# An attention layer over a graph: first layers of the radial network on quarters of TensorE, the odd aggregation in another bank

## The chip, the cores and the metric

The kernel runs on one core of a Trainium2 chip, in one launch. The metric is device time in microseconds (us), the median of repeated runs. A core has TensorE (PE, matrix products into PSUM banks), VectorE (DVE), ScalarE (ACT), GpSimd (POOL), SyncE (SP), and 16 DMA engines. Each engine takes its instructions in order; engines wait for one another through semaphores.

## The reference

400,000 edges, sorted by target node, join 12,500 nodes of 128 channels. For each edge a message is made, weighed by a softmax over the edges of its target, and summed there:

```
h = max(layernorm(x), 0)
msg_src = h @ w_src + b_src;  msg_dst = h @ w_dst
message = msg_src[src] + msg_dst[dst]
rad     = silu(silu(attr @ w1 + b1) @ w2 + b2) @ w3 + b3        # 32 -> 64 -> 64 -> 128
message = message * edge_weight * rad
message = message @ w_sep + b_sep                               # 8 heads, 16 for alpha, 16 for value
score   = sum(smooth_leaky_relu(alpha) * alpha_dot)             # per head
att     = segment_softmax(score, dst)
out     = x + segment_sum(value * att, dst) @ w_proj + b_proj
```

All of it is in float32.

## The kernel before

A first part (to about 235 us) makes the node tables `msg_src` and `msg_dst` and tables of indices and masks. A last part (from about 4935 us) divides the sums and projects them. Between them is the edge loop, which is the case here.

The loop goes over tiles of 512 edges: 832 tiles, one a step, written out in full (`stream`). Steps are grouped by 16 (`G`), and a group has one softmax. Two steps, an even and an odd one, make a pair `k`; the radial network is computed once a pair, for 1,024 edges. Each engine has its own function `step(g, j)` for step `j` of group `g`, and what stands there in order is the order on the engine. There is no scheduler. `there(t)` says whether tile `t` exists; `later(g, j, d)` is `d` steps on. The weighed sum of a tile comes 30 steps (`LAG`) after its message, when the softmax of its group is known. The names of the work:

- GpSimd: four gathers a step (L1057), each 128 rows of `msg_src` into `gath`, by indirect DMA. `gath` has four buffers, so the gathers of step t wait for the transposes of step t - 4 (`s_xT`).
- TensorE, in each step: transposes of `gath` into `xT_ps` (L1347) on top of the product that placed the target rows there the step before (`dst_part`, L1293); `aggregate` of tile t - 30 (L1304); every fourth step `scores` (L1314, four products side by side, 32 columns of the array each); the alpha half of the message, `a_ps` (L1366); its value half, `v_ps` (L1374); `dst_part` for the next step. Of the radial network, `z1` (L1270) is the first layer: one of its two products each step, behind the transposes. `z2` (L1276), the second layer, stands at the end of the even step, and `radial` (L1282), the third, in the odd step behind `a_ps`, as two products on upper and lower half of the array's rows.
- The weights `w1` and `w2` are laid out as blocks on a diagonal of 64x64 blocks with zeros elsewhere, so a full 128x128 product serves two sets of edges and half of the array multiplies by zero.
- ScalarE: `first` and `second` are the silu behind layers one and two, `measure` and `prepare_hotT` make the selection matrix for `dst_part`, `copy_values` empties `v_ps`, and `sil` (L1243) is the silu on `a_ps`.
- VectorE: `msgT` (L1176) multiplies the message by `rads`; `scale_rad` (L1122) makes `rads` from the third layer; `mark` (L1132, `hot`) makes the selection matrix for the aggregation, in even steps; `weigh` (L1145, `wval`) makes weight times value, twice in odd steps; `accumulate` (L1164, L1167, `run`) adds the aggregation into the running sums; `sil` (L1197); and the pieces of the softmax (`soft`), in even steps.

PSUM: `z_ps` has two banks, the first for layer one and the second for layer two. `rad_ps` has two banks for the third layer; `aggregate` writes the first 272 columns of the first of them in even steps and of the second in odd ones, and so `radial` has to wait until VectorE has taken the odd tile's sums (`s_run`).

## Time and profile before

| what | us |
|---|---|
| median of 3 runs (lowest, highest) | 5045.86 (5043.74, 5046.71) |
| the profiled execution | 5048.61 |
| its span, first to last instruction | 5046.1 |
| TensorE busy | 4810.6 (95%) |
| VectorE busy | 3892.4 (77%) |
| GpSimd busy | 3696.0 (73%) |
| ScalarE busy | 2640.2 (52%) |
| edge loop, first to last gather | 235.1 to 4822.9 |

Busy is the time in which an instruction of the engine ran. For TensorE, products are pipelined and the ends are modelled; the distance from one start to the next says more than the duration. For GpSimd, "issue" stands for idle time in which it waited for nothing that the profile shows. An engine that is idle, and is not the one that all wait for, costs nothing.

### The profile page before, as it was taken

What the parts mean: (1) busy time and instruction counts of PE and PEld (TensorE: products, weight loads), DVE (VectorE), ACT (ScalarE), POOL (GpSimd) and SP (SyncE); (2) the same over time, 40 slices, a digit from 0 to 9 for tenths busy, and PEclk for the clock granted to TensorE, in tenths of its full rate; (3) what the DMA queues carried; (4) which work ended last, traced back from release to release, by engine and by line L of the source; (5) the groups of instructions that cost most, each with busy time, mean ns of one, the idle gap of its engine ahead of it and who ended that gap; (6) DMA issues with size and microseconds to landing.
All of it is one profiled execution on the core that took longest, in us unless ns stands there. A gap on an engine that the chain in (4) does not pass through costs nothing. (4 is left out here: it accounts for less than half of the span.)

```text
span 5046.1 us, 92924 instructions
## 1 busy us (share of the span) xinstructions
PE 4810.6 (95%) x28995; PEld 3437.8 (68%) x28995; DVE 3892.4 (77%) x6981; ACT 2640.2 (52%) x3992; POOL 3696.0 (73%) x3491
## 2 busy tenths in 40 slices
PE   3599999999999999999999999999999999999975
PEld 2456777777777777777777777777777777777764
DVE  6547877878777787877877787787777778777777
ACT  2455555555555555555555555555555555555521
POOL 2377777777777777777777777777777777777716
PEclk9799999999999999999999999999999999999975
DMA  6666766666666666667666676766666666666635
GB/s 188 191 200 199 211 208 208 208 208 208 201 212 210 208 205 210 205 203 214 208 208 204 208 209 202 213 207 210 206 206 209 203 213 206 209 207 206 210 79 159
DMA packets 889683, 1019.25 MB, mean 202 GB/s; under 512 B 161781, under 2 KB 778009, under 8 KB 888864
## 3 DMA queue, kind: packets, MB, share of 16 engines
q1 hardware_dynamic: 758843, 774.32, 47.5%
q0 software_dynamic: 108784, 223.44, 18.1%
q10 hardware_dynamic: 21556, 15.50, 1.2%
q8 instruction: 233, 3.82, 0.3%
q14 instruction: 267, 2.18, 0.1%
HBM read 863.59 MB, written 152.34 MB: 201 GB/s over the span
## 5 line engine op out<-in xcount | busy, mean ns | idle before, releaser
L1057 POOL DMA_INDIRECT gath<-msg_src,idx x3328 | 3553.2, 1068 | 1064.6 <-issue 964.9
L1243 ACT ACTIVATE sil<-a_ps,ba 128x512 f32<-128x512 f32 x832 | 572.0, 688 | 1671.0 <-PE a_ps L1366 1670.2
L1374 PEld LDWEIGHTS v_ps<-wv,msgT 128*128 128x128 f32 x6656 | 835.4, 191 | 526.3 <-issue 526.3
L1304 PEld LDWEIGHTS rad_ps<-wval,hot 128*128 128x128 f32 x6656 | 905.3, 193 | 74.0 <-DVE wval L1145 30.5
L1304 PE MATMUL rad_ps<-wval,hot 128*128 128x136 f32 x6656 | 923.0, 282 | 27.8 <-DVE wval L1145 26.5
L1176 DVE TENSOR_TENSOR msgT<-xT_ps,rads 128x512 f32<-128x512 f32 x832 | 575.2, 691 | 455.9 <-PE xT_ps L1347 410.5
L1374 PE MATMUL v_ps<-wv,msgT 128*128 128x128 f32 x6656 | 924.1, 282 | 0.0
L1366 PE MATMUL a_ps<-msgT,wa 128*128 128x512 f32 x1664 | 878.9, 610 | 9.1 <-DVE msgT L1176 9.1
L1122 DVE SCALAR_TENSOR_TENSOR rads<-rad_ps,b,rows_bc 128x1024 f32<-128x1024 f32 x416 | 534.1, 1284 | 294.8 <-PE rad_ps L1282 294.8
L1293 PE MATMUL xT_ps<-hotT,win 128*128 128x256 f32 x3328 | 731.3, 342 | 0.0
L1197 DVE SCALAR_TENSOR_TENSOR sil<-a_ps,sil 128x512 f32<-128x512 f32 x832 | 568.8, 684 | 208.0 <-ACT sil L1243 207.8
L1228 ACT ACTIVATE vals<-v_ps 128x512 f32<-128x512 f32 x832 | 493.8, 594 | 339.9 <-PE v_ps L1374 321.3
L1293 PEld LDWEIGHTS xT_ps<-hotT,win 128*128 128x128 f32 x3328 | 481.1, 190 | 199.9 <-issue 199.9
L1145 DVE TENSOR_TENSOR wval<-vals,wT 128x544 f32<-128x544 f32 x832 | 596.5, 717 | 0.4 <-ACT wT L1240 0.4
L1270 PE MATMUL z_ps<-attr,w 128*128 128x256 f32 x1664 | 499.0, 382 | 29.8 <-DMA attr<-in_edge_attr_t 29.8
L1132 DVE TENSOR_TENSOR hot<-iota_row,rel_tab 128x1024 f32<-128x1024 f32 x416 | 505.7, 1216 | 0.0
L1347 PE MATMUL xT_ps<-ident,gath 128*128 128x128 f32 x3328 | 499.2, 272 | 0.0
L1219 ACT ACTIVATE apart<-rows_bc,row_below 128x1024 f32<-128x1024 bf16 x416 | 473.5, 1138 | 12.7 <-DMA win<-msg_dst 12.7
L1282 PE MATMUL rad_ps<-h,w 64*128 64x512 f32 x1664 | 470.6, 642 | 0.2 <-DVE run L1167 0.2
L1223 ACT ACTIVATE hotT<-apart 128x1024 fp32r<-128x1024 f32 x416 | 441.8, 1062 | 0.0
L1276 PE MATMUL z_ps<-h,w 128*128 128x512 f32 x832 | 426.8, 595 | 0.0
L1347 PEld LDWEIGHTS xT_ps<-ident,gath 128*128 128x128 f32 x3328 | 383.7, 140 | 0.0
(235 smaller groups left out, 4059.2 us busy)
## 6 DMA issues: line engine op xcount, KB each, us to landing
rows_bc<-edge_rows SPq DMA_DIRECT2D x416, 768.0 KB
win<-msg_dst SPq DMA_DIRECT2D x1664, 128.0 KB
sums<-run SPq DMA_DIRECT2D x416, 272.0 KB
attr<-in_edge_attr_t SPq DMA_DIRECT2D x1664, 32.0 KB
gath<-msg_src,idx POOLq DMA_INDIRECT x3328
msg_dst<-dst_parts SPq DMA_DIRECT2D x98, 128.0 KB, 2.1
pen_g<-pen_rows SPq DMA_DIRECT2D x208, 32.1 KB
mask_g<-mask_rows SPq DMA_DIRECT2D x208, 32.0 KB
```

Of the source, the lines that this page charges most:

```text
L1057: pool.indirect_dma_start(gath[:, u, s], None, msg_src, bass.IndirectOffsetOnAxis(ap=idx[:, j // 8, at:at + 1], axis=0)).then_inc(s_gath[u ...
L1122: dve.scalar_tensor_tensor(rads[:, j % 4:j % 4 + 2].rearrange("p n (i e) -> p (n i) e", i=2), rad_ps[:, :, :].rearrange("p n (i e) -> p (n ...
L1132: dve.tensor_tensor(hot[:, u:u + 2].rearrange("p n s q -> p (n s) q"), iota_row[:, :].unsqueeze(1).broadcast_to((P, 2 * SUB, P)), rel_tab[ ...
L1145: product = dve.tensor_tensor(wval[:, u], vals[:, slot], wT[:, :, at:at + H].unsqueeze(3).broadcast_to((P, SUB, H, HV)), ALU.mult)
L1176: dve.tensor_tensor(msgT[:, j % 2], xT_ps[:, :], rads[:, j % 4], ALU.mult).then_inc(s_msg, 1)
L1197: dve.scalar_tensor_tensor(sil[:, j % 8], a_ps[:, :], 0.25, sil[:, j % 8], ALU.mult, ALU.add).then_inc(s_al, 1)
L1243: act.activation(sil[:, j % 8], a_ps[:, :], ACT.Silu, bias=ba[:, :]).then_inc(s_sil, 1)
L1293: last = pe.matmul(xT_ps[:, cols], lhsT=win[:, j % U, i, n], rhs=hotT[:, j % 4, cols], start=(i == 0 and n == 0), stop=False, skip_group_c ...
L1304: last = pe.matmul(rad_ps[:, j % 2, AW * i:AW * (i + 1)], lhsT=hot[:, j % 4, s], rhs=wval[:, j % 4, s].rearrange("p h k -> p (h k)"), star ...
L1347: last = pe.matmul(xT_ps[:, s * P:(s + 1) * P], lhsT=gath[:, j % U, s], rhs=ident[:, :], is_transpose=True, start=False, stop=True, skip_g ...
L1366: pe.matmul(a_ps[:, :], lhsT=wa[:, :], rhs=msgT[:, q], start=True, stop=True).then_inc(s_a, 1)
L1374: last = pe.matmul(v_ps[:, s * P:(s + 1) * P], lhsT=msgT[:, q, s * P:(s + 1) * P], rhs=wv[:, :], start=True, stop=True)
```

## The change

- `z1` computes the whole first layer of a pair in one go, in the even step: four products on quarters of the array (64 rows by 64 columns), 256 columns of edges each, without the zero blocks. `z2` does the same for the second layer. Both stand behind the even step's aggregation, `z2` first.
- The outputs are laid out anew: each bank of `z_ps` holds layer one in columns 0 to 255 and layer two in columns 256 to 511. `h1` and `h2` swap their shapes, and the two silu of ScalarE read both banks.
- `radial` moves in the odd step from behind `a_ps` to behind the aggregation.
- The odd aggregation writes the second bank of `z_ps` instead of the second of `rad_ps` (`partial`). TensorE waits ahead of the aggregation for the running sums of the tile before, and in the odd step also for `first` of the next pair (`layers_read`), which has read that bank.
- ScalarE does `second` and then `first` in the even step, ahead of `sil`; both were in the odd one, on either side of it.
- VectorE does `scale_rad` ahead of the second `weigh` instead of behind it, and waits there for `rows_bc` too.

On TensorE, in the loop's middle. Before, from an even step's scores to the next odd step's `v_ps` (`rad_ps<-h,w` is the third layer, `rad_ps<-wval,hot` the aggregation, `z_ps<-attr,w` the first layer, `z_ps<-h,w` the second):

```order
L1314 MATMUL sc_ps<-sil,adot 32x512 x4
L1366 MATMUL a_ps<-msgT,wa 128x512
L1374 MATMUL v_ps<-wv,msgT 128x128 x4
L1276 MATMUL z_ps<-h,w 128x512
L1293 MATMUL xT_ps<-hotT,win 128x256 x4
L1347 MATMUL xT_ps<-ident,gath 128x128 x4
L1270 MATMUL z_ps<-attr,w 128x256
L1304 MATMUL rad_ps<-wval,hot 128x136 x4
L1366 MATMUL a_ps<-msgT,wa 128x512
L1282 MATMUL rad_ps<-h,w 128x512 x2
L1374 MATMUL v_ps<-wv,msgT 128x128 x4
```

and now, from an odd step's transposes to the next even step's `a_ps` (`z_ps<-wval,hot` is the odd aggregation):

```order
L1364 MATMUL xT_ps<-ident,gath 128x128 x4
L1321 MATMUL z_ps<-wval,hot 128x136 x4
L1299 MATMUL rad_ps<-h,w 128x512 x2
L1390 MATMUL a_ps<-msgT,wa 128x512
L1395 MATMUL v_ps<-wv,msgT 128x128 x4
L1310 MATMUL xT_ps<-hotT,win 128x256 x4
L1364 MATMUL xT_ps<-ident,gath 128x128 x4
L1321 MATMUL rad_ps<-wval,hot 128x136 x4
L1286 MATMUL z_ps<-h,w 64x256 x4
L1277 MATMUL z_ps<-attr,w 64x256 x4
L1331 MATMUL sc_ps<-sil,adot 32x512 x4
L1390 MATMUL a_ps<-msgT,wa 128x512
```

The two halves of the first layer and the second layer leave their places, and stand as two sets of four behind the aggregation of the even step; the third layer stands ahead of `a_ps`; the odd aggregation goes to `z_ps`.

On VectorE, the odd step, from one `msgT` to the next. Before:

```order
L1176 TENSOR_TENSOR msgT<-xT_ps,rads 128x512
L1145 TENSOR_TENSOR wval<-vals,wT 128x544
L1164 SCALAR_TENSOR_TENSOR run<-run,keep,rad_ps 128x136
L1167 SCALAR_TENSOR_TENSOR run<-run,keep,rad_ps 128x136
L1145 TENSOR_TENSOR wval<-vals,wT 128x544
L1122 SCALAR_TENSOR_TENSOR rads<-rad_ps,b,rows_bc 128x1024
L1197 SCALAR_TENSOR_TENSOR sil<-a_ps,sil 128x512
```

and now:

```order
L1178 TENSOR_TENSOR msgT<-xT_ps,rads 128x512
L1147 TENSOR_TENSOR wval<-vals,wT 128x544
L1166 SCALAR_TENSOR_TENSOR run<-run,keep,z_ps 128x136
L1169 SCALAR_TENSOR_TENSOR run<-run,keep,z_ps 128x136
L1124 SCALAR_TENSOR_TENSOR rads<-rad_ps,b,rows_bc 128x1024
L1147 TENSOR_TENSOR wval<-vals,wT 128x544
L1199 SCALAR_TENSOR_TENSOR sil<-a_ps,sil 128x512
```

`rads` and the second `wval` have changed places.

```diff
--- before.py
+++ after.py
@@ -874,6 +874,7 @@
             UA = 8
             AHEAD_A = UA - 1
             NPAIR = NTILE // 2
+            partial = (rad_ps[:, 0], z_ps[:, 1])
             X1, X2, XF = 2 * AW, 2 * AW + 32, 2 * AW + 64
             attr = tb("attr", [P, UA, P])
             win = tb("win", [P, U, 2, PARTS, C], f32r)
@@ -881,8 +882,8 @@
             idx = tb("idx", [P, 2, 2 * G], i32)
             gath = tb("gath", [P, U, SUB, C])
             hotT = tb("hotT", [P, 4, TE], f32r)
-            h1 = tb("h1", [P, 2, 2, P])
-            h2 = tb("h2", [P, 2 * CE])
+            h1 = tb("h1", [P, 2, CE])
+            h2 = tb("h2", [P, 2, 2, P])
             apart = tb("apart", [P, 4, CE])
             row_below = tb("row_below", [P, 1])
             spare = tb("spare", [P, 1])
@@ -1118,6 +1119,7 @@
                 def scale_rad(g, j):
                     t = G * g + j
                     k = t // 2
+                    dve.wait_ge(s_rows[k % 2], 80 * (k // 2) + 80)
                     dve.wait_ge(s_rad, k + 1)
                     dve.scalar_tensor_tensor(rads[:, j % 4:j % 4 + 2].rearrange("p n (i e) -> p (n i) e", i=2),
                                              rad_ps[:, :, :].rearrange("p n (i e) -> p (n i) e", i=2), b3[:, :],
@@ -1161,10 +1163,10 @@
                         before = rescaled[:, :]
                     if j % 2 == 0:
                         need(dve, s_rst[r // 2], 16 * (4 * g + j // R))
-                    dve.scalar_tensor_tensor(run[:, r, 0], before, keep[:, bass.ds(2 * a, 1)], rad_ps[:, j % 2, 0:AW],
+                    dve.scalar_tensor_tensor(run[:, r, 0], before, keep[:, bass.ds(2 * a, 1)], partial[j % 2][:, 0:AW],
                                              ALU.mult, ALU.add).then_inc(s_run, 1)
                     dve.wait_ge(s_run, 2 * a + 1)
-                    dve.scalar_tensor_tensor(run[:, r, 1], run[:, r, 0], keep[:, bass.ds(2 * a + 1, 1)], rad_ps[:, j % 2, AW:2 * AW],
+                    dve.scalar_tensor_tensor(run[:, r, 1], run[:, r, 0], keep[:, bass.ds(2 * a + 1, 1)], partial[j % 2][:, AW:2 * AW],
                                              ALU.mult, ALU.add).then_inc(s_run, 1)
 
                 def step(g, j):
@@ -1188,10 +1190,10 @@
                             weigh(*later(g, j, 1 - LAG))
                         if there(t - LAG):
                             accumulate(*later(g, j, -LAG))
+                        if there(t + 1):
+                            scale_rad(*later(g, j, 1))
                         if there(t + 2 - LAG):
                             weigh(*later(g, j, 2 - LAG))
-                        if there(t + 1):
-                            scale_rad(*later(g, j, 1))
                     if there(t):
                         dve.wait_ge(s_sil, t + 1)
                         dve.scalar_tensor_tensor(sil[:, j % 8], a_ps[:, :], 0.25, sil[:, j % 8], ALU.mult, ALU.add).then_inc(s_al, 1)
@@ -1206,12 +1208,15 @@
             def _(act):
                 def first(k):
                     act.wait_ge(s_z1, k + 1)
-                    act.activation(h1[:, :, :, :].rearrange("p i r e -> p r i e"), z_ps[:, 0, :].rearrange("p (r i e) -> p r i e", r=2, i=2),
-                                   ACT.Silu, bias=b1[:, :]).then_inc(s_h1, 1)
+                    act.activation(h1[:, :, :], z_ps[:, :, 0:CE], ACT.Silu, bias=b1[:, :]).then_inc(s_h1, 1)
 
                 def second(k):
-                    act.wait_ge(s_z2, k + 1)
-                    act.activation(h2[:, :], z_ps[:, 1, :], ACT.Silu, bias=b2[:, :]).then_inc(s_h2, 1)
+                    if k + 1 < NPAIR:
+                        act.wait_ge(s_z1, k + 2)
+                    else:
+                        act.wait_ge(s_z2, k + 1)
+                    act.activation(h2[:, :, :, :].rearrange("p i r e -> p r i e"), z_ps[:, :, CE:2 * CE].rearrange("p r (i e) -> p r i e", i=2),
+                                   ACT.Silu, bias=b2[:, :]).then_inc(s_h2, 1)
 
                 def measure(g, j):
                     k = (G * g + j) // 2
@@ -1231,8 +1236,11 @@
                     t = G * g + j
                     if there(t - 1):
                         copy_values(*later(g, j, -1))
+                    if j % 2 == 0 and there(t + 2):
+                        second(t // 2 + 1)
+                        if there(t + 4):
+                            first(t // 2 + 2)
                     if j % 2 and there(t + 1):
-                        second((t + 1) // 2)
                         prepare_hotT(*later(g, j, 1))
                     if group(g - 1) and j == 12:
                         n = g - 1
@@ -1241,8 +1249,6 @@
                     if there(t):
                         act.wait_ge(s_a, t + 1)
                         act.activation(sil[:, j % 8], a_ps[:, :], ACT.Silu, bias=ba[:, :]).then_inc(s_sil, 1)
-                    if j % 2 and there(t + 3):
-                        first((t + 3) // 2)
                     if group(g - 1) and j == 11:
                         n = g - 1
                         act.wait_ge(s_soft, KS * n + 17)
@@ -1262,24 +1268,35 @@
 
             @block.tensor
             def _(pe):
-                def z1(k, r):
+                def z1(k):
                     u = k % (UA // 2)
-                    if r == 0:
-                        pe.wait_ge(s_attr[u], 64 * (k // (UA // 2)) + 64)
-                        need(pe, s_h1, k)
-                    product = pe.matmul(z_ps[:, 0, CE * r:CE * (r + 1)], lhsT=w1[:, r], rhs=attr[:, 2 * u:2 * u + 2].rearrange("p i e -> p (i e)"),
-                                        start=True, stop=True)
-                    if r:
-                        product.then_inc(s_z1, 1)
-
-                def z2(k):
-                    pe.matmul(z_ps[:, 1, :], lhsT=w2[:, :], rhs=h1[:, :, :, :].rearrange("p i r e -> p (i r e)"), start=True, stop=True).then_inc(s_z2, 1)
-
-                def radial(k):
-                    pe.wait_ge(s_h2, k + 1)
+                    pe.wait_ge(s_attr[u], 64 * (k // (UA // 2)) + 64)
                     for n in range(2):
                         rows = slice(FC * n, FC * (n + 1))
-                        last = pe.matmul(rad_ps[:, n, :], lhsT=w3[rows, :], rhs=h2[rows, :], start=True, stop=True, tile_position=(FC * n, 0))
+                        for r in range(2):
+                            last = pe.matmul(z_ps[FC * r:FC * (r + 1), n, 0:CE], lhsT=w1[rows, r, rows],
+                                             rhs=attr[rows, 2 * u:2 * u + 2].rearrange("p i e -> p (i e)"), start=True, stop=True,
+                                             tile_position=(FC * n, FC * r))
+                    last.then_inc(s_z1, 1)
+
+                def z2(k):
+                    for r in range(2):
+                        rows = slice(FC * r, FC * (r + 1))
+                        for n in range(2):
+                            last = pe.matmul(z_ps[FC * n:FC * (n + 1), r, CE:2 * CE], lhsT=w2[rows, rows], rhs=h1[rows, n, :], start=True, stop=True,
+                                             tile_position=(FC * r, FC * n))
+                    last.then_inc(s_z2, 1)
+
+                def layers_read(k):
+                    if k + 1 < NPAIR:
+                        pe.wait_ge(s_h1, k + 2)
+                    else:
+                        pe.wait_ge(s_h2, k + 1)
+
+                def radial(k):
+                    for n in range(2):
+                        rows = slice(FC * n, FC * (n + 1))
+                        last = pe.matmul(rad_ps[:, n, :], lhsT=w3[rows, :], rhs=h2[rows].rearrange("p i r e -> p (i r e)"), start=True, stop=True, tile_position=(FC * n, 0))
                     last.then_inc(s_rad, 1)
 
                 def dst_part(g, j):
@@ -1301,7 +1318,7 @@
                     for i in range(2):
                         for r in range(2):
                             s = 2 * i + r
-                            last = pe.matmul(rad_ps[:, j % 2, AW * i:AW * (i + 1)], lhsT=hot[:, j % 4, s], rhs=wval[:, j % 4, s].rearrange("p h k -> p (h k)"),
+                            last = pe.matmul(partial[j % 2][:, AW * i:AW * (i + 1)], lhsT=hot[:, j % 4, s], rhs=wval[:, j % 4, s].rearrange("p h k -> p (h k)"),
                                              start=(r == 0), stop=(r == 1))
                     last.then_inc(s_agg, 1)
 
@@ -1347,16 +1364,23 @@
                             last = pe.matmul(xT_ps[:, s * P:(s + 1) * P], lhsT=gath[:, j % U, s], rhs=ident[:, :], is_transpose=True,
                                              start=False, stop=True, skip_group_check=True)
                         last.then_inc(s_xT, 1)
-                        if there(t // 2 * 2 + 4):
-                            z1(t // 2 + 2, q)
+                        need(pe, s_run, 2 * (t - LAG))
                         if q == 0:
                             pe.wait_ge(s_rads, t // 2 + 1)
+                        elif there(t + 1):
+                            layers_read((t + 1) // 2)
                     if group(g - 1):
                         small_read(g - 1, j)
                     if there(t - LAG):
                         aggregate(*later(g, j, -LAG))
                     if group(g - 1) and j in (6, 8, 14):
                         soft(g - 1, j)
+                    if q and there(t) and there(t + 1):
+                        radial((t + 1) // 2)
+                    if q == 0 and there(t) and there(t + 2):
+                        z2(t // 2 + 1)
+                    if q == 0 and there(t) and there(t + 4):
+                        z1(t // 2 + 2)
                     if j % 4 == 0 and there(t - 1):
                         scores(g if j else g - 1, j // 4 - 1 if j else 3)
                     if group(g - 1) and j == 12:
@@ -1364,24 +1388,19 @@
                     if there(t):
                         pe.wait_ge(s_msg, t + 1)
                         pe.matmul(a_ps[:, :], lhsT=wa[:, :], rhs=msgT[:, q], start=True, stop=True).then_inc(s_a, 1)
-                        if q and there(t + 1):
-                            need(pe, s_run, 2 * (t - LAG) + 2)
-                            radial((t + 1) // 2)
                         need(pe, s_vout, t)
                         if group(g - 1) and j == 12:
                             pe.wait_ge(s_wT, g)
                         for s in range(SUB):
                             last = pe.matmul(v_ps[:, s * P:(s + 1) * P], lhsT=msgT[:, q, s * P:(s + 1) * P], rhs=wv[:, :], start=True, stop=True)
                         last.then_inc(s_v, 1)
-                        if q == 0 and there(t + 2):
-                            z2(t // 2 + 1)
                         if there(t + 1):
                             dst_part(*later(g, j, 1))
-                for r in range(2):
-                    z1(0, r)
-                z1(1, 0)
+                z1(0)
+                pe.wait_ge(s_h1, 1)
                 z2(0)
-                z1(1, 1)
+                z1(1)
+                layers_read(0)
                 radial(0)
                 dst_part(0, 0)
                 stream(pe, step)
```

## Rows read from the trace of the kernel before

**Rows 1.** The page: engines, then costliest groups (busy, mean ns | idle before).

```profile
PE 4810.6 (95%) x28995; PEld 3437.8 (68%) x28995; DVE 3892.4 (77%) x6981; ACT 2640.2 (52%) x3992; POOL 3696.0 (73%) x3491
...
L1057 POOL DMA_INDIRECT gath<-msg_src,idx x3328 | 3553.2, 1068 | 1064.6 <-issue 964.9
...
L1243 ACT ACTIVATE sil<-a_ps,ba 128x512 f32<-128x512 f32 x832 | 572.0, 688 | 1671.0 <-PE a_ps L1366 1670.2
...
L1122 DVE SCALAR_TENSOR_TENSOR rads<-rad_ps,b,rows_bc 128x1024 f32<-128x1024 f32 x416 | 534.1, 1284 | 294.8 <-PE rad_ps L1282 294.8
```

**Rows 2.** Windows of 16 steps: length, then busy us (x instructions) by engine, clock, DMA.

```profile
401.15:488.10 86.95, 86.58 (x527) 60.99 (x526) 68.74 (x115) 47.61 (x70) 67.42 (x64) 1.00 0.69 207
2433.80:2522.30 88.50, 88.48 (x542) 62.92 (x541) 70.09 (x118) 48.79 (x70) 68.86 (x64) 1.00 0.68 208
```

**Rows 3.** Timeline of TensorE over a pair of steps: start, us, engine, line, what.

```profile
2499.02 1.06 PE L1314 MATMUL sc_ps<-sil,adot 128*32 128x512 f32 x8
2500.02 1.13 PE L1366 MATMUL a_ps<-msgT,wa 128*128 128x512 f32 x2
2500.98 1.05 PE L1374 MATMUL v_ps<-wv,msgT 128*128 128x128 f32 x8
2501.87 1.02 PE L1276 MATMUL z_ps<-h,w 128*128 128x512 f32 x2
...
2503.20 0.60 PE L1347 MATMUL xT_ps<-ident,gath 128*128 128x128 f32 x4
2503.64 0.60 PE L1270 MATMUL z_ps<-attr,w 128*128 128x256 f32 x2
2504.08 1.09 PE L1304 MATMUL rad_ps<-wval,hot 128*128 128x136 f32 x8
...
2505.00 1.02 PE L1366 MATMUL a_ps<-msgT,wa 128*128 128x512 f32 x2
...
2506.01 1.13 PE L1282 MATMUL rad_ps<-h,w 64*128 64x512 f32 x4
...
2507.07 1.16 PE L1374 MATMUL v_ps<-wv,msgT 128*128 128x128 f32 x8
2507.98 0.72 PE L1293 MATMUL xT_ps<-hotT,win 128*128 128x256 f32 x4
...
2508.54 0.60 PE L1347 MATMUL xT_ps<-ident,gath 128*128 128x128 f32 x4
```

**Rows 4.** Groups on GpSimd in 257.9 to 338.0, 401.15 to 488.1, 2433.8 to 2522.3.

```profile
L1057 POOL DMA_INDIRECT gath<-msg_src,idx x64 | 60.5, 946 | 22.4 <-issue 18.0 <-PE xT_ps L1347 4.3
...
L1057 POOL DMA_INDIRECT gath<-msg_src,idx x64 | 67.4, 1053 | 19.5 <-issue 18.3 <-PE xT_ps L1347 1.2
...
L1057 POOL DMA_INDIRECT gath<-msg_src,idx x64 | 68.9, 1076 | 19.6 <-issue 18.4 <-PE xT_ps L1347 1.2
```

**Rows 5.** Timeline of GpSimd and VectorE about two gathers that were held up.

```profile
2454.23 1.22 DVE L1132 TENSOR_TENSOR hot<-iota_row,rel_tab 128x1024 f32<-128x1024 f32 x1
...
2454.67 1.59 POOL L1057 DMA_INDIRECT gath<-msg_src,idx  x1 [0.30 <-issue]
...
2461.73 0.72 DVE L1145 TENSOR_TENSOR wval<-vals,wT 128x544 f32<-128x544 f32 x1
...
2462.14 1.12 POOL L1057 DMA_INDIRECT gath<-msg_src,idx  x1 [0.30 <-issue]
```

**Rows 6.** Timeline: transposes of step 28, and the first gather of step 32.

```profile
395.11 0.60 PE L1347 MATMUL xT_ps<-ident,gath 128*128 128x128 f32 x4
...
401.19 0.95 POOL L1057 DMA_INDIRECT gath<-msg_src,idx  x1 [0.30 <-issue]
```

**Rows 7.** Timeline of the last gather and its transposes; a DMA issue row.

```profile
4821.29 1.59 POOL L1057 DMA_INDIRECT gath<-msg_src,idx  x1 [0.30 <-issue]
...
4835.59 0.60 PE L1347 MATMUL xT_ps<-ident,gath 128*128 128x128 f32 x4
...
src_g<-src_s,chunk_c POOLq DMA_INDIRECT x13, 3.1
```

## The prediction

> **What bounds the kernel now.** I read the page's table of engines first. TensorE is busy for 95% of the span and its clock is full (PEclk 1.00) through the edge loop, so TensorE looks like the bound [rows 1, 2]. The page's costliest group says something else too: GpSimd's 3,328 gathers were busy 3553.2 us and sat idle 1064.6 us before them, and hardly any of that idle was a wait for TensorE [rows 1]. 3553.2 + 1064.6 = 4618 us, nearly the whole loop. So the question is how far apart these two are. The view of windows puts a group of 16 steps at 88.50 us in the steady part, with TensorE busy for 88.48 of it [rows 2]. The order on TensorE in the timeline shows no gap to speak of either: the even step runs from one set of transposes to the next with starts that follow each other by the length of the work [rows 3].
>
> GpSimd is next. A gather takes 0.95 us and 0.30 us pass to the next, so they start 1.25 us apart. Early in the loop, where no `mark` and no `weigh` run yet, 64 gathers (16 steps) fit into 80.1 us, which is their own pace, 64 x 1.25 = 80.0 [rows 4]. In the steady part some gathers are longer: one that begins while VectorE's `hot` (1.22 us) is running takes 1.59 us, one that begins in `wval` takes 1.12 us, and both end about 0.8 us after VectorE's instruction [rows 5]. So `hot` and `wval` hold gathers up. The 64 gathers of a steady group take 68.9 + 19.6 = 88.5 us, the same as TensorE [rows 4].
>
> Which of the two follows the other? Between 401.15 and 488.10 GpSimd was far behind its release: the gather at 401.19 was free to go when the transposes at 395.11 (four steps earlier, 0.60 us long) had ended, 5.5 us before [rows 6]. There nothing but VectorE held it up, and 64 gathers took 86.95 us [rows 2, 4]. In the steady part it is TensorE that comes late, and gathered data wait for it: the last gather starts at 4821.29 and its transposes at 4835.59, 14.3 us later [rows 7]. So TensorE is the bound at 88.5 us per 16 steps, and GpSimd, left alone, needs 86.95. The slack is 1.55 us, or 1.8%. That is the number this change runs into.
>
> **The change part by part, on TensorE.** Removed per pair of steps: two first-layer products (start 2503.64 to 2504.08, 0.44 us each, one in each step: 0.88) and one second-layer product. The latter is the difference between the stretch from `v_ps` to the transposes in the even step (2500.98 to 2503.20, 2.22) and in the odd one (2507.07 to 2508.54, 1.47), plus the 0.10 that `v_ps` is longer in the odd one: 0.85 [rows 3]. Together 1.73 us.
>
> Added per pair: two sets of four products on quarters of the array, 256 columns each. The trace has halves side by side by rows (the third layer: two products of 512 columns, 1.06 us from start to next start against 0.86 for one) and quarters side by side by columns (scores: four products of 512, 1.00 us against 0.86), but none by both [rows 3]. Bounds: all four at once, 0.44 us a set (a full product of 256 columns); two at once, 0.88; one after the other, 1.76. I take 0.44, since both nearest rows show full concurrency. So 0.88 for both sets.
>
> Changing the layout of the array costs something. Scores take 1.00 for 0.86 of work and the `a_ps` behind them 0.96 instead of 0.87 (2500.02 to 2500.98); the third layer takes 1.06 [rows 3]. I read this as 0.2 to 0.3 us for going there and back. The even step now has such a block behind its aggregation. In half of the even steps scores follow directly, and only a change between two such layouts is new; I take 0.30 in the others and 0.15 there, mean 0.22. The third layer moves from behind `a_ps` to ahead of it and pays what it paid.
>
> Net: 1.73 - 0.88 - 0.22 = 0.63 us a pair, 5.0 us per 16 steps. TensorE alone would go from 88.5 to 83.5.
>
> The Trainium skill, "TensorE: Matmul & The Clock Gate", Part 3, says that a weight load overlaps running products only when it goes to other rows of the array. By that the second pass of each quarter would wait some 0.1 us for its weights, 0.3 us a pair, and TensorE would stand at 86 rather than 83.5. The scores' block, eight passes in 1.00 us, leaves no room for it, so I do not take it.
>
> **Waits.** By the same rows the new steps come to 4.8 us each on TensorE. Even: transposes 0.44, aggregation 0.92, two z blocks 0.88 and 0.30 of changes, `a_ps` 0.87, `v_ps` 0.89, destination products 0.46. Odd: 0.44, 0.92, third layer 1.06, 0.87, 0.91, 0.56. The odd aggregation writes the bank that the first layer's second half uses, so it waits for ScalarE's `first` of the even step; the third layer waits for the same. ScalarE does `second` and `first` (about 0.69 each, as its instructions of 128x512 take [rows 1]) as soon as the z blocks are done, 2.4 us into the even step, and ends at 3.8; the odd aggregation comes at 4.8 + 0.44 = 5.2. Cover 1.4 us. ScalarE's `sil` is some 0.4 us later for it (ready at 3.4, free at 3.8), and behind it wait VectorE's `sil` and then `msgT` of the odd step, whose consumer `a_ps` has aggregation and third layer, 2 us, ahead of it. I cost all this at nothing; ScalarE is busy 48.79 of 88.5 us [rows 2]. If that cover were gone, each 0.1 us of it would cost 0.8 us per 16 steps. The new wait of the odd aggregation for the even `run` is covered by most of a step. The next even aggregation waits for the second `wval`, which moves behind `rads` (1.28 [rows 1]) and ends some 4.1 us behind the start of VectorE's odd step (1.28 and four pieces of 0.7), against 4.8 where it is wanted. VectorE is busy 70.09 of 88.5 [rows 2], so this cover holds except behind the softmax scans, where it is thin. SP's wait for `rads`, ahead of loading `rows_bc`, is released earlier than before. The wait for `rows_bc` that `scale_rad` gets is for data that ScalarE has already read.
>
> **The sum.** The loop takes the larger of TensorE's 83.5 and what GpSimd needs. GpSimd's instructions don't change, only when `hot` and `wval` strike them. Bounds: each of the 8 `hot` in a group now holds a gather up by 1.59 - 0.95 = 0.64 us; at none it would be 86.95 - 5.1 = 81.8, and at 1.22 - 0.14 = 1.08 each, the most that one can do (the gather of 1.59 began 0.78 before `hot` ended and lost 0.64), 86.95 + 3.5 = 90.5. I take 86.95, the one stretch in which GpSimd ran unhindered by TensorE with the same VectorE work. From step 32 on there are 800 steps, 50 groups: 50 x 1.55 = 78 us. Then there is the lead. The last gather starts at 4821.29 and its transposes 14.3 us later; if GpSimd is the bound, they start when the data land, for which an indirect load elsewhere took 3.1 us [rows 7]. That is another 11 us, once. The first steps and the 30 steps of drain at the end are as before: there gathers at 1.25 us, or VectorE, set the pace.
>
> 78 + 11 = 89 us. The profiled execution took 5048.6, which gives 4959.6; it stands 2.7 above the median of 5045.9, so I forecast 4957 us by the median, 1.8% faster. Of 5.0 us that TensorE saves per 16 steps, 3.4 should turn into a wait for gathers.
>
> **Rivals.**
> A: TensorE stays the bound, because with `wval` moved the gathers slip between VectorE's instructions. For it: `wval` now stands just ahead of `sil` and `msgT`, so `hot` comes at a fixed distance behind it, and gathers align behind whatever held them up. Against: 16 steps in 83.5 leave only 3.5 us for all holding, half of the 6.95 seen. Time: 50 x 5.0 = 250 less, 4796 us. The Trainium skill, "SBUF — State Buffer", Who interferes with whom, reports that `tensor_tensor` did not stall DMA work issued from GpSimd, which by itself would give this case; the 1.59 us gathers beside `hot` say otherwise, and the measurement decides.
> B: No change, GpSimd at 88.5 to 88.9: the holding is what it is now in the steady part, and only the lead comes back. 5035 to 5055.
> C, slower: GpSimd becomes the bound in a bad alignment. With TensorE waiting for landings, VectorE's instructions follow the gathers at a fixed distance, so a `hot` can fall on a gather every time. Place: the gather next to `hot`. From 88.7 us per 16 steps on it costs more than the lead gives back; at 90.5 it is 50 x 2.0 - 11 = 89 more, 5135; in the middle about 5090. Against: in both stretches seen the holding is near 0.64.
> D, slower: the change does not do what it says, quarters run two at a time. Then 1.73 - 1.76 - 0.22 = -0.25 a pair, 90.5 us per 16 steps, about 5146 us (50 x 2.0 more). Against: halves and column quarters each run fully side by side.
>
> **Chances.** Forecast (GpSimd sets 85.5 to 88.5) 60%, by itself 4885 to 5035; A 17%; B 7%; C 10%; D 6%. A measurement of this kernel tells about 0.2% from nothing. Faster: 60 + 17 = 77%; same 7%; slower 16%. The range takes in part of A and of C: 4825 to 5060.
>
> **What would show it.** In the windows a steady group of 16 steps takes about 87 us; TensorE has idle ahead of its transposes, ended by the gather's DMA, where it had none; gathers start 3 us or more behind their release, and their transposes start 3 to 4 us after the last of the four instead of 14. The two `z_ps` blocks take about 0.45 us each from first start to next. Wrong would be: a group at 83 to 84 with gathers still waiting for transposes (A); z blocks of 0.9 us (D); TensorE waiting for VectorE's `wval` or ScalarE's `h1` in every pair, which would mean that my covers are wrong.

## The result and the profile after

| | before | after |
|---|---|---|
| median, us | 5045.12 | 4847.06 (4841.88 to 4851.75) |
| span of the profiled execution | 5046.1 | 4846.4 |
| last gather starts | 4821.29 | 4632.32 |
| its transposes start | 4835.59 | 4639.58 |

The ratio is 0.9607 (95% interval 0.959 to 0.9624): 198 us or 3.9% faster. 4957 was forecast, 88 us faster. The direction is right, and the gain is 2.2 times what was forecast. The time lies in the stated range (4825 to 5060), but outside the 4885 to 5035 that the forecast gave for its own mechanism: the range holds it because it was widened for rivals A and C, which is luck.

The page of the changed kernel, engines and the groups that answer to [rows 1]:

```profile
PE 4539.7 (94%) x33155; PEld 3243.3 (67%) x33155; DVE 3874.6 (80%) x6981; ACT 2651.9 (55%) x3992; POOL 3524.4 (73%) x3491
...
L1058 POOL DMA_INDIRECT gath<-msg_src,idx x3328 | 3381.3, 1016 | 1045.9 <-issue 927.8
...
L1364 PE MATMUL xT_ps<-ident,gath 128*128 128x128 f32 x3328 | 506.6, 275 | 63.9 <-DMA gath<-msg_src,idx 62.8
```

Two things are new. TensorE waits for gathered rows ahead of its transposes, 62.8 us in all, where it waited for none. And the gathers themselves are shorter, 1016 ns in the mean against 1068. The same instructions on GpSimd cost 172 us less in all.

Windows of 84.65 us (columns as in [rows 2]):

```profile
2348.40:2433.05 84.65, 82.80 (x619) 58.78 (x618) 69.46 (x118) 49.24 (x70) 65.15 (x65) 1.00 0.73 217
3500.00:3584.65 84.65, 83.80 (x627) 59.74 (x626) 70.37 (x120) 49.02 (x70) 65.38 (x64) 1.00 0.73 218
```

64 gathers, 16 steps, fit into one. A group of 16 steps went from 88.5 to about 84.6 us, and TensorE, which had filled it, has 0.9 to 1.9 us to spare in it.

TensorE's order of an even step without scores and the odd one behind it (the counterpart of [rows 3]; L1286 is the second layer, L1277 the first):

```profile
2389.43 0.60 PE L1364 MATMUL xT_ps<-ident,gath 128*128 128x128 f32 x4
2389.87 1.09 PE L1321 MATMUL rad_ps<-wval,hot 128*128 128x136 f32 x8
2390.89 0.23 PE L1338 MATMUL rad_ps<-ends,head_of 128*8 128x32 f32 x2
2391.04 0.66 PE L1286 MATMUL z_ps<-h,w 64*64 64x256 f32 x8
2391.53 0.61 PE L1277 MATMUL z_ps<-attr,w 64*64 64x256 f32 x8
2392.07 1.12 PE L1390 MATMUL a_ps<-msgT,wa 128*128 128x512 f32 x2
2393.03 1.05 PE L1395 MATMUL v_ps<-wv,msgT 128*128 128x128 f32 x8
2393.84 0.71 PE L1310 MATMUL xT_ps<-hotT,win 128*128 128x256 f32 x4
2394.39 0.60 PE L1364 MATMUL xT_ps<-ident,gath 128*128 128x128 f32 x4
2394.83 1.09 PE L1321 MATMUL z_ps<-wval,hot 128*128 128x136 f32 x8
2395.85 1.13 PE L1299 MATMUL rad_ps<-h,w 64*128 64x512 f32 x4
```

The two blocks take 0.49 and 0.54 us: all four quarters run at once. The aggregation ahead of a block on parts of the array is 0.1 longer (1.02 instead of 0.92), and so is `a_ps` behind it (0.96 instead of 0.87).

### The profile page after: what moved, and what is told of

The parts are those of the page before. It is cut to its first block and busy times, and to the rows that moved or that the text cites. A ratio compares the mean times of both kernels' runs of the same rounds, so it can differ in the third digit from the quotient of the medians.

```text
span 4846.4 us, 101233 instructions
## 1 busy us (share of the span) xinstructions
PE 4539.7 (94%) x33155; PEld 3243.3 (67%) x33155; DVE 3874.6 (80%) x6981; ACT 2651.9 (55%) x3992; POOL 3524.4 (73%) x3491
## 5 line engine op out<-in xcount | busy, mean ns | idle before, releaser
L1058 POOL DMA_INDIRECT gath<-msg_src,idx x3328 | 3381.3, 1016 | 1045.9 <-issue 927.8
L1395 PEld LDWEIGHTS v_ps<-wv,msgT 128*128 128x128 f32 x6656 | 869.9, 191 | 421.6 <-issue 421.6
L1390 PE MATMUL a_ps<-msgT,wa 128*128 128x512 f32 x1664 | 932.5, 642 | 0.0
L1395 PE MATMUL v_ps<-wv,msgT 128*128 128x128 f32 x6656 | 880.9, 275 | 6.9 <-ACT wT L1248 6.9
L1218 ACT ACTIVATE h<-z_ps,b 128x512 f32<-128x512 f32 x416 | 285.6, 687 | 907.5 <-PE z_ps L1277 902.6
L1390 PEld LDWEIGHTS a_ps<-msgT,wa 128*128 128x128 f32 x1664 | 248.1, 188 | 527.2 <-issue 515.0
L1310 PE MATMUL xT_ps<-hotT,win 128*128 128x256 f32 x3328 | 599.8, 302 | 0.0
L1364 PE MATMUL xT_ps<-ident,gath 128*128 128x128 f32 x3328 | 506.6, 275 | 63.9 <-DMA gath<-msg_src,idx 62.8
L1321 PE MATMUL rad_ps<-wval,hot 128*128 128x136 f32 x3328 | 460.7, 282 | 26.7 <-DVE wval L1147 26.7
L1321 PE MATMUL z_ps<-wval,hot 128*128 128x136 f32 x3328 | 463.6, 283 | 1.3 <-DVE ends_h L1085 0.7
L1321 PEld LDWEIGHTS rad_ps<-wval,hot 128*128 128x128 f32 x3328 | 418.6, 192 | 30.5 <-DVE wval L1147 30.4
```

The lines of the kernel that those rows point to most:

```text
L1058: pool.indirect_dma_start(gath[:, u, s], None, msg_src, bass.IndirectOffsetOnAxis(ap=idx[:, j // 8, at:at + 1], axis=0)).then_inc(s_gath[u ...
L1310: last = pe.matmul(xT_ps[:, cols], lhsT=win[:, j % U, i, n], rhs=hotT[:, j % 4, cols], start=(i == 0 and n == 0), stop=False, skip_group_c ...
L1321: last = pe.matmul(partial[j % 2][:, AW * i:AW * (i + 1)], lhsT=hot[:, j % 4, s], rhs=wval[:, j % 4, s].rearrange("p h k -> p (h k)"), sta ...
L1364: last = pe.matmul(xT_ps[:, s * P:(s + 1) * P], lhsT=gath[:, j % U, s], rhs=ident[:, :], is_transpose=True, start=False, stop=True, skip_g ...
L1390: pe.matmul(a_ps[:, :], lhsT=wa[:, :], rhs=msgT[:, q], start=True, stop=True).then_inc(s_a, 1)
L1395: last = pe.matmul(v_ps[:, s * P:(s + 1) * P], lhsT=msgT[:, q, s * P:(s + 1) * P], rhs=wv[:, :], start=True, stop=True)
```

## The experiments

Two figures say most in what follows: the length of a group of 16 steps, from the count of gathers in a long window, and for how long gathers are held up in it. For the second I took every gather longer than 0.97 us between 1000 and 4500 us, its time over 0.946 (the length of an undisturbed one, [rows 4]), and the VectorE instruction that was running when it began. What a group takes beyond 64 x 1.25 = 80 us is either such held time or added idle time.

| kernel | median, us | ratio to before (interval) | group, us | held, us | of it by `hot` |
|---|---|---|---|---|---|
| before | 5045 | | 88.5 | 8.1 | 5.1 |
| after | 4847.06 | 0.9607 (0.959, 0.9624) | 84.6 | 4.7 | 1.4 |
| x1, old VectorE order | 4844.48 | 0.9597 (0.9581, 0.9613) | 84.6 | 4.6 | 1.8 |
| x3, three gathers | 4762.75 | 0.9439 (0.9423, 0.9455) | 83.3 | - | - |
| x4, before with TensorE lighter | 4870.71 | 0.9651 (0.9635, 0.9667) | 84.9 | 5.0 | 2.8 |
| x5, full products, new places | 5026.64 | 0.9963 (0.9949, 0.9978) | 88.2 | 7.4 | 2.2 |
| x7, `hot` with one input, after | 4787.08 | 0.949 (0.9474, 0.9506) | 83.4 | 3.4 | 0 |
| x7b, the same, before | 5046.29 | 0.9999 (0.999, 1.0009) | 88.5 | 4.3 | 0 |
| x2, after with TensorE lighter by two | 4904.15 | 0.9714 (0.9696, 0.9732) | 85.8 | 5.7 | 2.8 |
| z2, after with TensorE lighter by one | 4898.99 | 0.9714 (0.9697, 0.973) | 85.6 | 5.6 | 2.9 |
| x8, `hot` in two | 4829.79 | 0.9568 (0.9552, 0.9584) | 84.1 | 4.2 | 1.6 |
| z1, `hot` and `wval` in two | 4783.59 | 0.9478 (0.9462, 0.9493) | 83.3 | 3.3 | 1.3 |

**x1: VectorE's order.** The changed kernel with

```diff
-                        if there(t + 1):
-                            scale_rad(*later(g, j, 1))
                         if there(t + 2 - LAG):
                             weigh(*later(g, j, 2 - LAG))
+                        if there(t + 1):
+                            scale_rad(*later(g, j, 1))
```

> The changed kernel, with VectorE's second wval back ahead of rads. Theory 1 (how long hot and wval hold gathers up follows from the fact that landings now time VectorE, whatever the order on VectorE): a group of 16 steps stays at 84 to 85.5 us, time 4835 to 4890. Theory 2 (the new place of wval, just ahead of sil, is what lets gathers slip past hot): hot holds each gather up by about 0.64 us again, a group takes about 87 us, time about 4950. Theory 3 (GpSimd hardly matters, TensorE is the bound): within 10 us of 4847.

4844.48: the new order on VectorE has no part in the gain. Theory 2 falls. The time suits theories 1 and 3 alike; x3 parts them.

**x3: TensorE's own pace.**

```diff
-                    for s in range(SUB):
+                    for s in range(SUB - 1):
                         at = SUB * (j % 8) + s
```

with the transposes reading `gath[:, j % U, min(s, SUB - 2)]` and the counts of the waits made 48.

> The changed kernel with three gathers a step instead of four (the fourth quarter of a tile reuses the third's rows, so a quarter of the edges get wrong source rows); TensorE does all its work. It shows TensorE's own pace. By my sum TensorE needs 83.5 us per 16 steps, time about 4790; if the 80 us of starts delayed ahead of the transposes in the trace are the whole of what gathers cost, 83.1 us and 4770. If TensorE is the bound already (theory 3): 4840 to 4850.

4762.75. In 3500 us there are 2018 gathers, 48 to a group, so a group takes 83.25 us, and TensorE is busy for 3486.75 of the 3500:

```profile
1000.00:4500.00 3500.00, 3486.75 (x26062) 2488.38 (x26055) 2927.14 (x4961) 2063.64 (x2942) 2461.16 (x2018) 1.00 0.70 208
```

This is TensorE's own pace, 83.5 by my sum. So the changed kernel pays 84 us for its gathers, some 68 of it in the groups (50 x 1.35), and theory 3 falls. This run has less DMA traffic too; x7 below, with all four gathers, comes out at nearly the same group.

**x4: the same saving without the change.** The kernel before with

```diff
-                        for n in range(PARTS):
+                        for n in range(1):
                             last = pe.matmul(xT_ps[:, cols], ...
```

> The kernel before with two of the four destination products of each step left out (the second part of the target rows is missing from the messages), which takes 2 x 0.118 us off TensorE a step, 3.8 us per 16 steps, without moving anything: TensorE would need 84.7. Theory 1 (timing by landings lowers the holding by itself): 84.7 to 85.5 us, time 4845 to 4890. Theory 2 (the order on VectorE does it): GpSimd keeps its need of about 87 us, time 4950 to 4960. If GpSimd were no limit at all: 4848.

4870.71, a group of 84.9, 0.2 above what TensorE would need. Nothing was moved, the order on VectorE is the old one, only TensorE has 3.8 us less to do, and gathers that needed 86.95 by my reading now fit into 84.9:

```profile
1000.00:4500.00 3500.00, 3490.47 (x20931) 2436.04 (x20930) 2852.56 (x4861) 2009.61 (x2885) 2696.01 (x2638) 1.00 0.73 216
```

TensorE is busy for all but 9.5 us of this and never waits for a gather in it, so what gathers need is at most 84.9. Each `hot` still strikes a gather, 8.0 a group, but holds it 0.35 us instead of 0.64. In x3, where gathers have far more time than they need, `hot` holds 8.0 a group as well, for 0.95 us each. This is the run that takes my step apart.

**x5: full products at the new places.** `z1` and `z2` as 128x128 products with the zero blocks, `h1`, `h2` and `z_ps` laid out as before, all else as in the changed kernel:

```diff
-                            last = pe.matmul(z_ps[FC * n:FC * (n + 1), r, CE:2 * CE], lhsT=w2[rows, rows], rhs=h1[rows, n, :], ...
+                    last = pe.matmul(z_ps[:, 1, :], lhsT=w2[:, :], rhs=h1[:, :, :, :].rearrange("p i r e -> p (i r e)"), ...
```

> The changed kernel with the first two layers as full 128x128 products (two of 256 columns, one of 512, with the zero blocks, and the old layout of z_ps, h1, h2), at their new places. It parts quarters from places. By my sum quarters save 0.63 us a pair net, and places nothing: a group near 88.5 us, time 5030 to 5045. If the new places (no wait of the third layer for the sums, more work ahead of a_ps) carry a part of the gain: each 1 us per 16 steps makes 52 us, and 4950 would be two such.

5026.64: the new places, the bank and the new waits give 19 us together (11 to 26 by the interval), a little more than I expected, and the quarters give the other 180.

**x7 and x7b: take away the conflict at `hot`.** The comparison of two SBUF inputs becomes a sum over one, from tile 4 on:

```diff
+                    if a >= 4:
+                        dve.tensor_reduce(hot_sum[:, :], hot[:, u:u + 2].rearrange("p n s q -> p (n s) q"), mybir.AxisListType.X, ALU.add).then_inc(s_hot, 1)
+                        return
```

> The changed kernel with hot's comparison (two inputs in SBUF) replaced, from tile 4 on, by a sum over the same 128x1024 elements (one input in SBUF) of about the same length; hot keeps its first values, so the aggregation is wrong. In the changed kernel's trace hot holds gathers up for 1.4 us per 16 steps. Theory G (these holds are part of the time, GpSimd is the bound): a group falls from 84.6 to about 83.2 us, where TensorE's own 82.9 comes in, time 4765 to 4800, and gathers are held up next to wval and the scans alone. Theory T (holds only fill slack of GpSimd, TensorE and its jitter are the bound): no change, 4840 to 4850.

4787.08, 60 us less, and no gather is held at `hot` any more. The sum takes VectorE 1.21 us where the comparison took 1.22, so VectorE's load did not change. Theory G stands: in the changed kernel the holding is part of the time.

> The same replacement in the kernel before, where hot holds gathers up for 5.1 us per 16 steps. Both theories: TensorE is the bound there and the holds are slack taken up, so 5040 to 5050; the gathers' idle ahead, ended by the transposes, or the holds at wval grow by what hot no longer takes. If the holds were a need of GpSimd, as my forecast read them, the first stretch that ran free (401 to 488 us) would be shorter: 64 gathers in about 82 us instead of 86.95.

5046.29. In the kernel before, 5.1 us of holding by `hot` went from each group and the time did not move. Of it, 2.2 us came back as more holding at `wval` (3.8 instead of 1.5), and the rest, with 0.9 us that one of the softmax scans no longer held, as idle. Gathers between 1000 and 4500 us:

```profile
L1058 POOL DMA_INDIRECT gath<-msg_src,idx x2531 | 2559.2, 1011 | 941.9 <-issue 768.4 <-PE xT_ps L1351 173.5
```

The wait for transposes is 173.5 us here and 51.0 in the kernel before. So there the holding was how GpSimd waited for TensorE's pace, not what it needed. The stretch of 401 to 488 us, which I had taken for free running, shrank too: 16 steps of gathers took 85.0 us instead of 86.9 (I had put 82 to it).

**x2 and z2: TensorE lighter still.** The changed kernel with `range(1)` for `range(PARTS)` as in x4 (x2), or with `range(PARTS - (i == 0))` (z2).

> The changed kernel with two of the four destination products of each step left out (the second part of the target rows is missing from the messages): TensorE's own pace falls from 82.9 to 79.1 us per 16 steps, GpSimd's instructions stay. It shows what GpSimd needs when it is the bound alone. Theory G: 83.5 to 84.6 us, time 4790 to 4847. Theory T: TensorE's saving shows in full, as far as 64 gathers at 1.25 us (80 us) allow, 4650 to 4700.

> The changed kernel with one of the four destination products of each step left out (a part of the target rows is missing), TensorE's own pace at about 81.4 us per 16 steps. If GpSimd's need grows steadily as TensorE gets further ahead: about 4875. If the alignment is set anew by each spacing: anywhere from 4780 to 4910, and the trace shows the time in how long hot holds gathers.

4904.15 and 4898.99: TensorE has 3.8 or 1.9 us less to do in a group, and the kernel is more than 50 us slower than the changed one. Both theories were wrong on x2. z2, asked after it, is not the 4875 of a steady growth; it lies in the range that I had given for a new alignment (4780 to 4910), a wide one. Where the time goes is in the trace. TensorE's waits for gathers between 1000 and 4500 us, in the changed kernel, then in x2:

```profile
PE xT_ps L1364 <- DMA gath<-msg_src,idx: 40.0, 56, 1.8
```

```profile
PE xT_ps L1364 <- DMA gath<-msg_src,idx: 181.9, 144, 4.8
```

And gathers beside `hot` in x2 (timeline of GpSimd and VectorE):

```profile
2399.40 1.22 DVE L1134 TENSOR_TENSOR hot<-iota_row,rel_tab 128x1024 f32<-128x1024 f32 x1
...
2399.57 1.86 POOL L1058 DMA_INDIRECT gath<-msg_src,idx  x1 [0.31 <-issue]
2401.74 1.42 POOL L1058 DMA_INDIRECT gath<-msg_src,idx  x1 [0.30 <-issue]
...
2409.76 1.22 DVE L1134 TENSOR_TENSOR hot<-iota_row,rel_tab 128x1024 f32<-128x1024 f32 x1
...
2410.98 0.95 POOL L1058 DMA_INDIRECT gath<-msg_src,idx  x1 [0.30 <-issue]
```

The first `hot` starts 0.17 us ahead of a gather and costs it 0.91; the second falls between the starts of two and costs nothing. In the changed kernel `hot` holds 5.7 of 64 gathers, for 0.25 us each; in x2 it holds 4.2, for 0.68. The sum closes: 80 us and 5.7 of holding are 85.7, and a group takes 85.8. This was rival C's mechanism, in a weaker form than the 88.7 us and more that it was given. One less product or two made little difference (85.6 and 85.8), so it is no steady function of TensorE's lead. What decides into which alignment the loop falls, I have not settled, and x2 was not run with the holding at `hot` taken away.

**x8 and z1: shorter instructions.**

```diff
-                    dve.tensor_tensor(hot[:, u:u + 2]..., iota_row..., rel_tab[:, bass.ds(SUB * a, 2 * SUB)]..., ALU.is_equal).then_inc(s_hot, 1)
+                    for i in range(2):
+                        part = dve.tensor_tensor(hot[:, u + i], iota_row..., rel_tab[:, bass.ds(SUB * (a + i), SUB)]..., ALU.is_equal)
+                    part.then_inc(s_hot, 1)
```

and in z1 `wval` in two halves of `SUB` as well.

> The changed kernel with hot made by two instructions of 512 elements instead of one of 1024; result unchanged. VectorE pays about 0.06 us for each of 8 more instructions per 16 steps. Theory G: a gather that starts inside is held at most half as long, hot's 1.4 us per 16 steps fall to about 0.7, time about 4810. Theory T: no change.

> hot and wval both made by two instructions of half the length. Theory G: another 20 us below the kernel with hot split (4830), 4800 to 4815. If VectorE's 1 us more per 16 steps or a worse alignment decides: 4830 or more.

4829.79 and 4783.59, against 4810 and 4800 to 4815 expected. z1 beats the changed kernel by 63 us and is 5.2% faster than the one before; it computes all that they compute. Its group of 83.3 us is TensorE's own pace from x3, and its waits for gathers are down to 17.1 us in the whole span, against 62.8. The direction of both is theory G's; the parts are not: in x8 `hot` held as long as before (1.6 us a group) and `wval` less. The sum of all holding fell, its shares were not where I put them, so that a gather is held less because the instruction is shorter is not shown; a new alignment could do the same. The price on VectorE was higher than expected too: two halves of `hot` take 0.15 us more than the whole (2 x 0.682 against 1.216), not 0.06. The two were compared with the kernel before on their chips, not with the changed kernel side by side.

**Eight runs on two slow chips.** x11 and y1 (the changed kernel unaltered), x12 and y2 (`hot` in two), x9 and y3 (z1's kernel), x10 and y4 (z2's) ran on chips where the kernel before took 6096 and 6135 us.

> The changed kernel once more, unaltered, so that the split kernels can be compared with it on one chip: 4840 to 4852.

> hot made by two instructions of 512, again, on the same chip as the changed kernel. Theory G (shorter instructions can hold a gather less): 10 to 25 us below the changed kernel. If the 17 us between them came from the chips and not from the split: within 5 us.

> hot and wval both made by two instructions of half the length; result unchanged. Theory G: a gather that starts inside wval is held at most half as long as well; of 0.9 us per 16 steps that wval still costs about half goes, another 20 us below the kernel with hot split, toward TensorE's own pace: 4800 to 4815. Against it: 16 more instructions on VectorE, about 1 us per 16 steps; if that or a worse alignment decides, 4830 or more.

> The changed kernel with one of the four destination products of each step left out (a part of the target rows is missing), TensorE at about 81.4 us per 16 steps, half-way to the kernel with two left out, which took 4904. If GpSimd's need grows steadily as TensorE gets further ahead: about 4875. If the alignment of gathers and hot is set anew by each spacing of the instructions, it can fall anywhere from 4780 to 4910. If the extra time came from something else that lacks two products (a DMA, a wait of VectorE): the trace will show waits there in place of held gathers.

> The changed kernel, unaltered, as the base of the two split kernels on the same chip: 4840 to 4852.

> hot made by two instructions of 512 elements. Theory G (shorter instructions hold a gather less, and the holding is part of the time): 10 to 25 us below the changed kernel. If the 17 us found between them came from two chips: within 5 us.

> hot and wval both made by two instructions of half the length. Theory G: another 20 us below the kernel with hot split, 4800 to 4815. If VectorE's 1 us more per 16 steps or a worse alignment decides: 4830 or more.

> The changed kernel with one of the four destination products of each step left out (a part of the target rows is missing), TensorE's own pace at about 81.4 us per 16 steps. If GpSimd's need grows steadily as TensorE gets further ahead: about 4875. If the alignment is set anew by each spacing: anywhere from 4780 to 4910, and the trace shows the time in how long hot holds gathers. If the time came from another wait, that wait is in the trace in place of held gathers.

They took 6196.69, 6166.94, 6256.95 and 6187.89 on the one, 6296.60, 6227.02, 6377.58 and 6276.62 on the other: the changed kernel is slower there than the one before, by 1.6% (1.0122 to 1.0197) and 2.6% (1.0226 to 1.0288), and z1's by 2.8 and 3.9%. Every time that was forecast for them missed by more than 1200 us. Of the differences, `hot` in two took 30 and 70 us less than the changed kernel (the first within the intervals), where 10 to 25 had been expected; z1's kernel took 60 and 81 us more, the other way than on the other chips; z2's took 9 and 20 less, within the intervals. What paces the kernel there is something else (last section), so I draw nothing on the theories from them; but neither the change nor z1's edit is a gain on every chip.

## Why the prediction was wrong

- TensorE's part was right. Forecast: 5.0 us less per 16 steps, 83.5. x3: 83.25, with three gathers; 83.4 in x7, with four. By parts: the blocks 0.49 and 0.54 instead of 0.44 each, the changes of layout 0.2 instead of 0.30 where no scores follow, the third layer without its gap. The Trainium skill's rule on weight loads ("TensorE: Matmul & The Clock Gate", Part 3), which the forecast names and does not take, would have given 86; the blocks leave no room for such waits (0.49 us for two passes of 256 columns, where one full product of 256 took 0.44).
- That GpSimd would come next, eat the lead and make TensorE wait for landings was right, and only the size of it was wrong. The step was: "I take 86.95, the one stretch in which GpSimd ran unhindered by TensorE with the same VectorE work". In the changed kernel it is 84.6. This term, 50 x 1.55 = 78 us, should have been 50 x 3.9 = 195. With the lead's 7 that makes 202, and 198 were measured. Of what TensorE saves per 16 steps, 1.4 us turned into a wait for gathers, not 3.4.
- Why it was wrong: a held gather is not a fixed price. x7b shows that while TensorE set the pace at 88.5 the holds were slack (take them away, and other holds and idle take their place), and x4 shows that with TensorE faster the same instructions fit into 84.9. How I read it: `hot` starts when TensorE's pace lets it, gathers run ahead until a `hot` catches them, and the hold is as long as the two paces differ. The eight holds a group of 0.35, 0.64 and 0.95 us in x4, before and x3 agree; it was not tried by itself. In the stretch that I read, gathers hardly waited for a semaphore, but VectorE ran at TensorE's pace, so they were not unhindered: TensorE was busy for 86.58 of those 86.95 us [rows 2], a row that I had in front of me. I had 81.8 to 90.5 as bounds and took a point measured in the wrong regime.
- A right reading would not have given 84.6 either. The changed kernel and its variants take 83.3 to 85.8 us a group, as gathers are held for 3.3 to 5.7 us in it, and nothing that I found in the trace of the kernel before told which.
- The lead gave 7 us (14.3 to 7.3 from last gather to transposes), not 11: a landing takes longer here than the 3.1 us of the indirect load that I went by. Wherever TensorE waited for gathers, 83 times in the changed kernel, its transposes started 2.9 to 7.3 us behind the start of the last gather, 5.3 in the median.
- The covers held. Between 1000 and 4500 us TensorE waits for nothing but gathers (40.0 us) and two copies of the softmax (8.5 us); neither `wval` nor `h1` appears.
- Rival A had the time nearer (4796) for half of the reason: `hot` does hold less, but not through the new place of `wval` (x1). Rival B is out by the group of 84.6. Rival C did not come with this change; x2 and z2 show a mild form of it. Rival D is out by the blocks' 0.5 us.

## What to carry to other kernels

When an engine that hardly waits for a semaphore is nonetheless held up by another's instructions, as gathers are here by `hot` and `wval`, the lengths of its own say little of what it needs: they stretch to fill the slack while something else sets the pace. To learn its need, make the engine that sets the pace lighter and look at the time (x4), before a saving is costed against it. Where such a conflict is part of the time, halving the instructions that do the holding is a cheap edit to try (z1, 63 us); it is one to measure, since the parts did not move as reasoned and two other chips showed a loss.

## What the runs showed of the hardware

- Quarters of TensorE, 64x64, run all four at once in float32: two passes of four products with 256 columns take 0.49 us, against 0.44 for one full product of 256, and a switch between the whole array and parts costs about 0.1 us each way.
- A comparison or product on VectorE with both inputs in SBUF holds a GpSimd gather that starts inside it until about 0.8 us behind its end (0.81 in the gather of 1.86 us above, 0.81 and 0.81 in [rows 5]); a sum with one input of the same size (x7) holds none. The sum is another instruction as well as one input less. The Trainium skill, "SBUF — State Buffer", Who interferes with whom, says that two SBUF inputs contend with GpSimd instructions that read SBUF, and the 1.59 to 1.9 us gathers agree, if the reading of the indices is what is held (that was not tried alone); it also reports a probe in which `tensor_tensor` did not stall DMA work, and infers why; these indirect gathers it does stall: with `hot` on one input the changed kernel is 60 us faster. It says too that `tensor_reduce` never contends on trn2, and x7 agrees.
- Less work on the busiest engine made the kernel slower: x2 and z2, over 50 us.
- On two chips everything took longer, and signals from one engine reached the next late. The waits of y1 (the changed kernel), longest in total first:

```profile
POOL gath L1058 <- issue: 1085.4, 2919, 6.4
ACT h L1218 <- remote: 1028.0, 145, 12.3
...
DVE msgT L1178 <- remote: 640.1, 212, 6.0
...
POOL gath L1058 <- remote: 573.9, 237, 3.5
```

"remote" stands where no signal of the trace explains the end of a wait; the changed kernel has no such row on the other chips. There `msgT` starts 0.04 us behind its transposes; in y1 it starts more than 3 us behind in 13% of the cases between 1000 and 4500 us in which VectorE was free (10% in x11). The granted clock is lower there too: 0.90 and 0.91 in the mean for the changed kernel and 0.94 for the one before, against 0.97 and 0.98 on the other chips, and TensorE is busy for 5153.0 us in y1 where it was for 4539.7. How much of the time is the clock and how much the late signals was not parted. Why these chips are so, why the changed kernel loses more by it, and what the kernel before waits for on them, stays open; no trace of the kernel before was taken there.
